# Spreading bias rows and gates with TensorE instead of DMA, a split that casts its rest, and the order that goes with them

## Time and profile before

| | |
|---|---|
| median of 3 runs | 299.56 us (298.98 to 306.13) |
| the profiled execution | 298.25 us, of which the span of the page is 296.4 us |
| mean granted TensorE clock | 0.977 |
| busy: TensorE, VectorE, ScalarE, GpSimd | 258.8, 215.8, 215.0, 218.5 us |
| DMA traffic | 24.74 MB, 41363 packets |

### The profile page before, as it was taken

One profiled execution on the slowest core, in us unless ns is written; L12 is line 12 of the kernel. 1 busy time (PEld: TensorE's weight loads), 2 busy tenths in 40 slices (PEclk: granted clock), 3 DMA queues, 4 the chain that ended last, 5 costly groups with the idle time before them and its releaser, 6 DMA issues.

```text
span 296.4 us, 8985 instructions
## 1 busy us (share of the span) xinstructions
PE 258.8 (87%) x3172; PEld 161.9 (55%) x3172; DVE 215.8 (73%) x463; ACT 215.0 (73%) x462; POOL 218.5 (74%) x393
## 2 busy tenths in 40 slices
PE   2837997999996779768899999999999999999995
PEld 2524544555645566545666766656464646455553
DVE  2399997798845636835572788867889999999923
ACT  2133587698887387476769888898979797878992
POOL 6896757467887588897599889898989988882120
PEclk9986999999999799997999999999999999999999
DMA  4569142523346033453113322221123222221002
GB/s 136 165 176 253 49 126 67 137 80 92 104 124 164 5 80 96 138 134 92 31 46 83 91 59 56 59 54 29 47 65 81 56 66 52 73 67 29 4 3 71
DMA packets 41363, 24.74 MB, mean 83 GB/s; under 512 B 4960, under 2 KB 39656, under 8 KB 41320
## 3 DMA queue, kind: packets, MB, share of 16 engines
q1 hardware_dynamic: 37144, 17.71, 23.2%
q10 hardware_dynamic: 3792, 5.41, 6.3%
q0 software_dynamic: 384, 1.05, 1.2%
HBM read 7.56 MB, written 0.54 MB: 27 GB/s over the span
## 4 chain that ended last, share of the span: by engine, by line
PE 54%; DVE 10%; DMA 9%; POOL 8%; ACT 8%; issue 7%; SPq 3%; POOLq 0%; ACTq 0%; DVEq 0%
PE ps L768 11%; PE ps L726 10%; PE ps L725 8%; PE ps L696 7%; DVE neg_max L1042 6%; PE ps L794 5%; DMA q_stack<-max_rows_split 4%; ACT probs L899 4%; PE ps L761 4%; PE ps L856 3%; POOL heads_normed L529 2%; SPq L490 2%; DMA q_stack<-q_parts 2%; PE ps L867 2%; PE ps L804 1%
## 5 line engine op out<-in xcount | busy, mean ns | idle before, releaser
L1042 DVE TENSOR_REDUCE neg_max<-ps 128x2 f32<-128x512 f32 (+1 forms) x256 | 160.4, 682 | 32.1 <-PE ps L725 31.2
L899 ACT ACTIVATE probs<-ps 128x512 f32<-128x512 f32 x256 | 134.5, 608 | 14.7 <-PE ps L726 12.5
L725 PE MATMUL ps<-k_stack,q_stack 62*128 62x256 bf16 (+1 forms) x640 | 63.7, 257 | 10.1 <-DMA q_stack<-q_parts 4.7
L726 PE MATMUL ps<-q_stack,k_stack 64*128 64x256 bf16 (+1 forms) x640 | 59.3, 252 | 6.2 <-DMA q_stack<-max_rows 2.5
L768 PE MATMUL ps<-probs,v_cols 128*32 128x256 f32 x768 | 52.3, 385 | 0.7 <-ACT probs L899 0.6
L725 PEld LDWEIGHTS ps<-k_stack,q_stack 62*128 62x128 bf16 x640 | 31.3, 96 | 32.1 <-issue 10.8
L726 PEld LDWEIGHTS ps<-q_stack,k_stack 64*128 64x128 bf16 x640 | 30.1, 95 | 29.1 <-issue 9.5
L768 PEld LDWEIGHTS ps<-probs,v_cols 128*32 128x32 f32 x768 | 20.2, 109 | 18.2 <-issue 8.1
L518 POOL CAST max_parts<-neg_max 128x16 bf16<-128x16 f32 (+2 forms) x34 | 6.8, 201 | 26.6 <-DVE neg_max L1042 26.2
L933 ACT ACTIVATE q_f<-ps,vec 128x256 f32<-128x256 f32 x32 | 15.1, 479 | 7.1 <-PE ps L794 6.7
L1068 DVE RECIPROCAL inv_sum<-ps 128x32 f32<-128x32 f32 x20 | 7.1, 355 | 18.0 <-PE ps L696 17.9
(11 more groups left out here) (120 smaller groups left out, 425.3 us busy)
## 6 DMA issues: line engine op xcount, KB each, us to landing
k_stack<-k_parts SPq DMA_DIRECT2D x120, 64.0 KB, 2.1
q_stack<-q_parts SPq DMA_DIRECT2D x114, 64.0 KB, 2.1
gates<-gates_dram ACTq DMA_DIRECT2D x4, 384.0 KB, 3.8
w<-in_w ACTq DMA_DIRECT2D x2, 512.0 KB, 4.6
rows<-in_rows ACTq DMA_DIRECT2D x1, 704.0 KB, 6.7
q_stack<-max_rows_split SPq DMA_DIRECT2D x44, 4.0 KB
w<-in_w ACTq DMA_DIRECT2D x1, 576.0 KB, 5.5
ctx_t<-in_ctx_t SPq DMA_DIRECT2D x4, 128.0 KB, 2.9
```

The costliest lines, as they stand in the source:

```text
L725: return nc.tensor.matmul(out, queries, keys, start=True, stop=True)
L726: return nc.tensor.matmul(out, keys, queries, start=True, stop=True)
L899: nc.scalar.activation(probs[:, n % PROB_BUFS, :], ps[bank_of["score", p, b, i]][:, :], ACT.Exp, scale=SCALE).then_inc(of(st), 1)
L1042: nc.vector.tensor_reduce(dst, src, AX.X, ALU.max, negate=True).then_inc(of(st), 1)
```

## The change

- **Split.** Step 0 now makes the float32 rest (the same subtraction as L499), waits for it, and casts it into `part[1]`; step 1 only makes `part[2] = rest - part[1]`. Three instructions per split as before, one of them a cast instead of a subtraction. `split_r` now has room for every sequence.
- **Bias rows.** Row 0 of a zeroed tile `one_row` gets the 8 bias rows by one 4 KB DMA; two matmuls of 512 columns with a one-column selector spread it to all partitions, and ScalarE copies the two banks out.
- **Gates.** Gate biases come by their own small DMA. `gates_small` becomes a zeroed 128-partition tile; eight matmuls of 384 columns (one for each sequence and half) spread its rows, and ScalarE copies them out. The store and the four broadcast reads are gone, and `gate_fold` and `add_mlp` wait for the copies.
- **Loads.** x and weight groups 2, 1 and 3 (512, 576, 256 and 256 KB) leave ScalarE's queue and are issued by SP right after the inputs of sequences 2 and 3, before SP's first `stack_k`. Groups 4 and 5 (512 KB each) stay on ScalarE's queue: group 4 just before TensorE's `mod` step, group 5 just after its `gate` step and the first max copy behind it; before, they stood in phase 1 and at the start of phase 2.
- **Order.** `ORDER`, `BANK_OF` and `COUPLED` are new; 192 steps are coupled instead of 185. At the start TensorE has k0 k1 rope0 q0 k2 rope1 k3 v1 rope2 q1 q2 rope3, the bias rows with v2 between them, then the first max step; before it had q0 k0 rope0 q1 k1 rope1 rope2 q2 k2 and then the first max step. VectorE has `turn_k` of sequence 3 before its first maximum, which it had after the sixteenth.
- A second, unreachable copy of two branches on GpSimd is removed.

The core of the diff:

```diff
-LOADS = ("x", "rows", 2, 1, 3, 4, 5)
-SPREADS = B
+BIAS_ROWS = 2
+LOADS = (4, 5)
...
-        "4": ("act", only([("keep_gates", 0, 0)] + [("spread", 0, i) for i in range(SPREADS)], first)),
+        "4": ("pe", [("spread", 0, i) for i in range(2)]),
+        "8": ("act", [("take_spread", 0, i) for i in range(2)]),
+        "+": ("pe", only([("bias_rows", 0, i) for i in range(BIAS_ROWS)], first)),
+        "-": ("act", only([("take_bias_rows", 0, i) for i in range(BIAS_ROWS)], first)),
...
             if i == 0:
                 engine.wait_ge(*part_ready(kind, p, b, 0))
-                ops.tensor_tensor(part[1], full, part[0], ALU.subtract).then_inc(of(step), 1)
+                link(ops.tensor_tensor(rest, full, part[0], ALU.subtract))
+                ops.tensor_copy(part[1], rest).then_inc(of(step), 1)
             else:
-                link(ops.tensor_tensor(rest, full, part[0], ALU.subtract))
                 engine.wait_ge(*part_ready(kind, p, b, 1))
                 ops.tensor_tensor(part[2], rest, part[1], ALU.subtract).then_inc(of(step), 1)
-                engine.wait_ge(*done(*step))
...
             load_batch(sp, 1)
+            sp.wait_ge(one_row_cleared, 1)
+            sp.dma_start(one_row[0:1, :], a["rows"].partition_broadcast(1)).then_inc(rows_loaded, 16)
+            sp.dma_start(gate_rows[...], a["gate_rows"].partition_broadcast(2 * B)).then_inc(gate_rows_loaded, 16)
             sp.wait_ge(gathered[0], NT * 16)
             load_batch(sp, 2)
             load_batch(sp, 3)
+            sp.dma_start(x[...], a["x"]...).then_inc(x_loaded, 16)
+            for group in (2, 1, 3):
+                load_w(sp, group)
...
             nc.gpsimd.memset(mean_mat[:, :], 1.0 / (D * D)).then_inc(mean_set, 1)
+            nc.gpsimd.memset(one_row[:, :], 0.0).then_inc(one_row_cleared, 1)
+            nc.gpsimd.memset(gates_small[...], 0.0).then_inc(gates_cleared, 1)
             clear_v(FIRST[1]).then_inc(first_v_cleared, 1)
...
                 elif kind == "gate_fold":
-                    pool.wait_ge(gates_spread[b], 16)
-                    pool.wait_ge(rows_loaded, 16)
+                    pool.wait_ge(*done("take_spread", 0, b, 1))
+                    pool.wait_ge(*done("take_bias_rows", 0, FIRST[1], BIAS_ROWS - 1))
...
+                elif kind == "spread":
+                    pe.wait_ge(const_loaded, 16)
+                    pe.wait_ge(gates_cleared, 1)
+                    pe.wait_ge(*done("take_gate", 0, 0, 0))
+                    row = 2 * b + i
+                    last = nc.tensor.matmul(out[:, 0:3 * D], ident[:, row:row + 1].broadcast_to([P, P]),
+                                            gates_small[...], start=True, stop=True)
+                elif kind == "bias_rows":
+                    pe.wait_ge(const_loaded, 16)
+                    pe.wait_ge(rows_loaded, 16)
+                    n = len(R_NAMES) * D // BIAS_ROWS
+                    last = nc.tensor.matmul(out[:, 0:n], ident[:, 0:1].broadcast_to([P, P]),
+                                            one_row[:, n * i:n * (i + 1)], start=True, stop=True)
...
+                elif kind == "take_spread":
+                    act.wait_ge(*done("spread", p, b, i))
+                    nc.scalar.activation(gates[:, 2 * b + i, ...], ps[...][:, 0:3 * D], ACT.Copy)
+                elif kind == "take_bias_rows":
+                    act.wait_ge(*done("bias_rows", p, b, i))
+                    nc.scalar.activation(rows[:, n * i:n * (i + 1), :], ps[...][:, :], ACT.Copy)
```

More of the change, by code:

```diff
@@ L153 @@
[L153 to L157, removed]
@@ L246, in signal @@
             return own[kind]
-        if kind in ("stack_k", "stack_q", "gather", "load", "keep_gates", "spread"):
+        if kind in ("stack_k", "stack_q", "gather", "load"):
             return None
@@ L386, in build @@
         max_placed = [[sem(f"max_placed{g}{i}") for i in range(B)] for g in range(4)]
-        gates_stored = sem("gates_stored")
-        gates_spread = [sem(f"gates_spread{i}") for i in range(B)]
+        gate_rows_loaded = sem("gate_rows_loaded")
+        one_row_cleared = sem("one_row_cleared")
+        gates_cleared = sem("gates_cleared")
         out_stored = sem("out_stored")
@@ L490, in place_parts, with split_part @@
                     queue.dma_start(stack[slot::ROW_SLOTS, b, :, :], parts_of(kind, b)[part]).then_inc(sem_, 16)
-        def split_part(engine, ops, link, rest, kind, p, b, i):
+        def split_part(engine, ops, link, kind, p, b, i):
             part, full = parts_of(kind, b), q_f[:, b, 0 if kind == "q" else 1, :]
+            rest = split_r[:, b, 0 if kind == "q" else 1, :]
             step = ("split_" + kind, p, b, i)
@@ L612, in _ @@
                 elif kind in ("split_k", "split_q"):
-                    split_part(pool, nc.gpsimd, link, split_r[:, int(kind[-1] == "k"), :], kind[-1], p, b, i)
+                    split_part(pool, nc.gpsimd, link, kind[-1], p, b, i)
                 elif kind == "split_max":
@@ L823, in _ @@
                                             w[:, W_AT["ada2"]:W_AT["ada8"] + 1:3, :], start=True, stop=True)
+                elif kind == "spread":
[4 more added lines that the diff above has]
+                    last = nc.tensor.matmul(out[:, 0:3 * D], ident[:, row:row + 1].broadcast_to([P, P]),
+                                            gates_small[:, :, :].rearrange("p k c -> p (k c)"), start=True, stop=True)
+                elif kind == "bias_rows":
+                    pe.wait_ge(const_loaded, 16)
+                    pe.wait_ge(rows_loaded, 16)
+                    n = len(R_NAMES) * D // BIAS_ROWS
+                    last = nc.tensor.matmul(out[:, 0:n], ident[:, 0:1].broadcast_to([P, P]), one_row[:, n * i:n * (i + 1)],
+                                            start=True, stop=True)
                 elif kind == "gamma":
@@ L1063, in _ @@
                 elif kind in ("split_k", "split_q"):
-                    split_part(dve, nc.vector, link, split_first[:, int(kind[-1] == "k"), :], kind[-1], p, b, i)
+                    split_part(dve, nc.vector, link, kind[-1], p, b, i)
                 elif kind == "normalise":
@@ L1108, in _ @@
                     dve.wait_ge(*done("gate", 0, 0, 0))
-                    dve.wait_ge(rows_loaded, 16)
-                    nc.vector.tensor_tensor(gates_small[:, :, :],
+                    dve.wait_ge(gate_rows_loaded, 16)
+                    dve.wait_ge(gates_cleared, 1)
+                    nc.vector.tensor_tensor(gates_small[0:2 * B, :, :],
                                             ps[bank_of["gate", 0, 0, 0]][0:2 * B, 0:3 * D].rearrange("p (a b) -> p a b", a=3),
-                                            rows[0:2 * B, R_AT["gate1"]:R_AT["gate3"] + 1, :], ALU.add).then_inc(of(st), 1)
+                                            gate_rows[:, :, :], ALU.add).then_inc(of(st), 1)
                 elif kind == "quant_abs":
@@ L1169, in host_layout @@
             "vec": np.stack([v[n] for n in V_NAMES], axis=1),
-            "rows": np.concatenate([r[n] for n in R_NAMES])}
+            "rows": np.concatenate([r[n] for n in R_NAMES]),
+            "gate_rows": np.concatenate([r[f"gate{n}"] for n in (1, 2, 3)])}
 def constants():
```

150 lines of the change are left out of this document (66 added, 84 removed).

## The result

The changed kernel took 303.51 us (median of 4 runs, 301.23 to 305.37) beside 299.48 us for the kernel before: ratio 1.0129, 95% interval 1.0077 to 1.0181. A second measurement with more runs gave 1.0082 (1.0044 to 1.0121). So it is about 1% slower, some 3 us, where I had forecast 2.8 us less.

What follows compares the result with a forecast made beforehand. TensorE was taken as the bound from 180 to 280 us, with 12.3 us idle from 80 to 142. Terms 5.9 - 2.2 - 8.1 + 2.0 - 1.4 - 0.5 + 1.5 = -2.8 gave 296.8 us against 299.56; range 290 to 304.

Steps and rivals of the forecast that it cites:

- Rival B: Loads on SP's queue delay the stacks of sequence 0; first maximum near 28 us, kernel slower at 302 us; chance 0.15.
- The start: Up to VectorE's first maximum: clears, the moved turn_k and 1600 KB ahead of the stacks cost +1.5 us (+0.5 to +5).
- point of decision: At the start: the slower rival holds if the first k_stack DMA lands after 24 us.
- spreads, work: TensorE: eight float32 matmuls of 384 columns at 0.74 us each add +5.9 us (bounds +3.9 and +5.9).
- idle and clock from 40 to 280 us: Hidden spreads -2.2, DMA relief of two stalls and their low clock -8.1, waits at the loads' new place +2.0 us.
- coupling and split: Seven fewer TensorE steps, -1.4 us, and a cast replacing a subtraction in the splits, -0.5 us.
- Spreads: Gates spread by TensorE: +5.9 us of matmuls, of which -2.2 hides in idle stretches of phase 1.
- DMA traffic: From 80 to 142 us: without the bulk transfers two stalls shrink and the clock returns, -8.1 us (bounds -8.1 and 0).
- rival A: The holes of 80 to 142 us close, giving 11.5 us there; kernel at 292.5 us; chance 0.25.
- Where the two loads went: Groups 4 and 5, issued from just before the mod matmuls, cost 1 us of waiting each: +2.0 us (0 to 7.1).
- Split: GpSimd saves 10.2 us by casts instead of subtractions, which TensorE feels little: -0.5 us (bounds +0.5 and -2).
- seven steps of coupling: Where TensorE is the bound: 192 coupled steps instead of 185 save 7 x 0.2 us, -1.4 us.

Runs made afterwards that it cites:

- d2_loads_early: Kernel before, with only x and weight groups 2, 1 and 3 issued by SP ahead of its first k_stack: 305.32 us, ratio 1.0193 to the kernel before.
- g1: b1 with weight groups 4 and 5 issued late again (93.3 and 107.3 us): ratio 0.9973 to the kernel before.
- g2: Kernel before, with only weight groups 4 and 5 moved early (59.6 and 65.2 us): ratio 0.9896 to the kernel before.
- b1: Changed kernel with x and weight groups 2, 1, 3 back on ScalarE's queue and VectorE's three splits in the old form: 297.77 us, ratio 0.9936.
- d1_split_alone: Kernel before, with only the new split, on VectorE and GpSimd alike: ratio 1.0053 to the kernel before.
- a1: Changed kernel with x and weight groups 2, 1 and 3 back on ScalarE's queue, each issued a little before use: ratio 1.0021 to the kernel before.

## Why the prediction was wrong

303.51 us lies within the wide range that I gave (290 to 304), but the kernel is slower where my sum said faster. Of the rivals, B with its 302 us comes nearest.

**The step that failed** is "The start": "I take **+1.5** for the first maximum (bounds +0.5 and +5)". It measured +5.66, outside its bound, and `d2_loads_early` alone +5.8 us of time. I asked only when the stacks land and left out the gathers, which come over GpSimd's queue and which TensorE needs, in order, first; their row stood among mine, read for its issue and not for its landing. I also took 238 GB/s for the loads from a stretch that carried stacks and loads together; the last of them landed near 24 us, not near 21. Yet the first `k_stack` DMA, issued behind them at 16.19, landed at 22.5, and only the last placement of the stacks near 28.5. And "VectorE does `turn_k` of sequence 3, 2 x 0.42 us" counted the moved step but not the cast just before it, which went from 0.29 to 2.3 us and held the parts behind it.

**Rival B** had the place right (first maximum "near 28 us": 28.93) and the price too low: it added 3.0 us to the sum where the term was off by 4.2. What I put against it, "VectorE's own chain ends near 24.5 us anyway", counted as cover; it was a second late chain. It had the loads right too (through at 24.6; near 24). But its point of decision was not met: the first `k_stack` DMA was to land after 24 us and landed at 22.5, ahead of the last of the loads. That its 28 us came out is in part luck, as it had neither the gathers nor the cast.

The Trainium skill's rule that I had weighed (DMA: Bandwidth & Descriptors, Queues, rings and completion order) spoke against the change and points the right way, but the order within a ring cannot be all of it. Around 16 to 20 us of the kernel after, placements on SP's queue, behind the loads, took 6.3 to 7.2 us to land, placements on ScalarE's queue 6.3 to 6.7, and gathers on GpSimd's 6.7 to 7.3: all three alike. Nor do landings keep that order, as the same section says too: the first placement landed ahead of the last load.

**A balance of the two profiled spans** (+2.8 us), by my own terms:

| term | predicted | measured |
|---|---|---|
| start | +1.5 | +5.7 |
| spreads, work | +5.9 | +6.0 (eight at 1.49/2 us) |
| idle and clock from 40 to 280 us | -8.3 (with what hides) | -9.8 |
| coupling and split | -1.9 | rest: +0.9 |

The third row is -2.2 - 8.1 + 2.0 of the prediction against TensorE's idle time in the four windows, 20.05 us before and 12.38 after, and the clock: 62 x 0.06 = 3.7 us got back, 40 x 0.04 = 1.6 newly lost. That loss lies from 40 to 50 us (clock 0.83), ahead of the two moved loads, and so belongs to the start. The windows are fixed stretches and do not hold quite the same work in both kernels, so the table is an estimate. The last row is what is missing to +2.8, not a measurement of its own; it also holds the stretch from the first maximum to 40 us, where TensorE runs at a clock of 0.83 once more, and the end.

**Spreads: right in size.** The chain gives two of them in

```profile
94.20 1.49 PE ps L827 x4
```

and the group of these instructions by form is `x16`, 510 ns for one. Net of what hides I had 3.7 us; removing their width gives 2 to 3, so rather more hides than I had. ScalarE's copies, 8 x 0.49 us, stayed in every run, so their price is not shown.

**DMA traffic: right in sum, wrong in part as to cause.** About eight us came, as rival A had it too. But moving the loads alone gives 3.1 us in the old order, where idle time falls by 3.5 us and nothing comes back of the 3.4 us of clock in my sum. And in `g1`, with the loads late again, TensorE idles 6.2 us from 80 to 142 us: most of the 7.3 us was closed by the rest of the change (the new order, the new matmuls that fill it, the gates' broadcast reads gone, the lighter split), which no run takes apart. The largest wait left from 80 to 142 us in the kernel after is 0.61 us:

```profile
127.66 0.38 PE L723 MATMUL ps<-k_stack,q_stack 62*128 62x128 bf16 x4 [0.61 <-DVE heads_t_gated L1080]
```

**Where the two loads went: half of it.** Issued at 55.4 and 62.1 us; a new unit then waits once:

```profile
67.03 0.40 PE L723 MATMUL ps<-k_stack,q_stack 62*128 62x256 bf16 x4 [1.05 <-DMA k_stack<-k_parts]
```

1.05 us instead of the 2.0 that I had for both. From 50 to 80 us the clock stays at 1.00.

**Split: wrong as a number of its own.** Its price depends on the order around it: 0.5 to 1.3% slower in the old one, 0.7 to 0.9% faster in the new. GpSimd's 10 us less were right.

**Left open.** Why the lighter split slows the old order was not traced to a wait. What the order alone gives was not measured by itself: there is no run with the new order and all else old. The seven steps of coupling (-1.4) were tested by no run. The two fastest complete versions, g2 and b1, belong to two different orders; b1 has the two loads early already, so their gains cannot be added.

## What to carry to other kernels

Before bulk loads are moved ahead of a latency-bound start, list every transfer of those microseconds on every queue, with who waits for each landing; a free slot on one queue says nothing about the others. If two chains end within a microsecond of each other, undoing one can show nothing: undo both. A stall that a transfer ends can be closed by moving the transfer or by other changes around it, and only trying each alone tells which; here the smallest edit, two loads moved from the stall to a full stretch, was worth more than the whole change.

## What the runs showed of the hardware

**A VectorE cast stands still while GpSimd clears memory.** 128x256 float32 to bfloat16 takes 0.29 us; it took 1.12 to 2.44 us in all eight cases in these traces where it met clears of 0.96 us, and ended just after one of them each time. In `d1_split_alone`, where the first cast ends after the first of two clears:

```profile
15.16 1.12 DVE L498 CAST k_parts<-split_r 128x256 bf16<-128x256 f32 x1
15.18 0.95 POOL L504 MEMSET q_stack<- 128x1024 f32 x1
18.42 0.29 DVE L498 CAST q_parts<-split_r 128x256 bf16<-128x256 f32 x1
```

The subtraction that the cast replaced shows 0.41 to 0.43 us beside the same clears, and in `b1` 0.86 us beside a subtraction of GpSimd. The position arithmetic of the start does the same: one step takes 0.88 us where the added clears push the clear of `k_stack` beside it, and 0.17 with the added clears late. The Trainium skill (SBUF — State Buffer, Who interferes with whom) says that VectorE and GpSimd share one pair of ports as an exclusive lock: a VectorE instruction in a two-port mode, which copies and casts can enter, blocks fully against GpSimd, and one with two inputs from SBUF only against a GpSimd instruction that reads SBUF. By that rule the cast waits for the clears and the subtraction doesn't; the rows agree on both. They do not settle who gets the lock: the skill gives it to whoever starts first, and five of the eight casts start 0.1 to 0.4 us ahead of the first clear, at the end of a gather's issue on GpSimd, and are held all the same. No run varied the ports, so the cause is the skill's and the durations are the traces'.

**The same float32 work costs twice at the low clock.** A bias-row step, two instructions of 512 columns, takes 2.08 us in a1 and 1.02 in b1: 1.2 against 2.4 GHz, with a granted clock of 0.50 from 24 to 30 us in a1 and of 1.00 from 22 to 28 us in b1. TensorE had idled 2.99 us ahead of that work in a1, but 2.64 us in b1 as well, where the clock fell only from 28 us on. The kernel before has such a stretch as well (21 to 27 us); what it costs depends on the work that stands in it.
